# Position attention in a two-layer kernel: softmax in two halves of rows, value products one unit behind score products, later residual sums, pairwise sums in the last turn

## What is computed

```python
qkv = jnp.einsum('sbh,oh->sbo', ln1, qkv_weight)        # 16 query heads, 4 key/value heads, 16 wide
scores = jnp.einsum('bgqsd,bgtd->bgqst', qb, kb) * scale
scores = jnp.where(causal, scores, jnp.finfo(scores.dtype).min)
attn = jax.nn.softmax(scores, axis=-1)
ao = jnp.einsum('bgqst,bgtd->bgqsd', attn, vb)          # s, t in 0..7, t <= s
proj = jnp.einsum('sbh,oh->sbo', ao, proj_weight)
h1 = hidden_states + proj
ln2 = _layer_norm(h1, ln2_weight, ln2_bias)
logits = x @ router_weight
```

## Time and profile before

| | us |
|---|---|
| median of 3 executions | 1807.87 |
| lowest and highest | 1803.91, 1808.4 |
| the profiled execution, its own time | 1806.29 |
| its span in the trace | 1804.5 |
| granted TensorE clock, mean | 0.967 of full speed |
| busy: PE, DVE, ACT, POOL | 92%, 55%, 36%, 28% |

### The profile page before, as it was taken

One profiled execution on the slowest core, in us unless ns is written; L12 is line 12 of the kernel. 1 busy time (PEld: TensorE's weight loads), 2 busy tenths in 40 slices (PEclk: granted clock), 3 DMA queues, 4 the chain that ended last, 5 costly groups with the idle time before them and its releaser, 6 DMA issues. The chain is left out here.

```text
span 1804.5 us, 32036 instructions
## 1 busy us (share of the span) xinstructions
PE 1662.5 (92%) x10572; PEld 1279.3 (71%) x10572; DVE 996.0 (55%) x2525; ACT 643.2 (36%) x1913; POOL 504.8 (28%) x655
## 2 busy tenths in 40 slices
PE   8999899999999978669779999997999997999998
PEld 6777677777778745568768888886666665656555
DVE  6545457787777876895532222215888885322221
ACT  3333255454555465345531111112444443111110
POOL 3222210000000067775153333315455541100000
PEclk9999899999999999889789999999999999999999
DMA  7776500000000000000413233323111100000000
GB/s 192 133 150 114 97 13 13 13 13 13 12 12 1 1 16 1 18 24 28 151 47 100 94 117 94 95 58 100 31 29 30 32 27 1 12 12 12 23 12 24
DMA packets 92268, 88.52 MB, mean 49 GB/s; under 512 B 11456, under 2 KB 82048, under 8 KB 91776
## 3 DMA queue, kind: packets, MB, share of 16 engines
q1 hardware_dynamic: 73392, 56.63, 13.1%
q0 software_dynamic: 6912, 18.88, 3.8%
q10 hardware_dynamic: 11856, 11.66, 1.9%
HBM read 46.64 MB, written 23.20 MB: 39 GB/s over the span
## 5 line engine op out<-in xcount | busy, mean ns | idle before, releaser
L845 ACT ACTIVATE probs<-psS,nm 128x256 f32<-128x256 f32 x256 | 119.1, 470 | 182.5 <-DVE nm L878 182.5
L1764 DVE COPY YE<-e_psY 128x512 f32<-128x512 f32 x40 | 27.7, 692 | 227.7 <-PE e_psY L1712 227.7
L1702 PE MATMUL e_psH<-e_XT,w 128*128 128x256 f32 x640 | 144.8, 379 | 0.0
L1712 PE MATMUL e_psY<-w,e_HT 128*128 128x256 f32 x640 | 144.5, 379 | 0.0
L876 DVE TENSOR_REDUCE mx<-psS 128x2 f32<-128x512 f32 x128 | 87.9, 686 | 84.0 <-PE psS L766 81.7
L1712 PEld LDWEIGHTS e_psY<-w,e_HT 128*128 128x128 f32 x640 | 121.6, 190 | 16.5
L766 PE MATMUL psS<-Rec,QT 128*128 128x256 f32 (+1 forms) x512 | 132.3, 381 | 0.9 <-ACT QT L833 0.9
L1740 ACT ACTIVATE e_HT<-e_psH 128x512 f32<-128x512 f32 x80 | 47.7, 597 | 235.9 <-PE e_psH L1702 235.9
L1702 PEld LDWEIGHTS e_psH<-e_XT,w 128*128 128x128 f32 x640 | 118.6, 190 | 14.5
L1670 POOL DMA_INDIRECT XE<-token_rows,held x80 | 76.0, 950 | 184.6 <-PE e_psX L1689 167.1
L1023 POOL TENSOR_TENSOR prodS<-QKV 128x256 f32<-128x256 f32 x112 | 84.8, 792 | 140.0 <-ACT QKV L1191 113.7
(11 more groups left out here) (285 smaller groups left out, 3559.4 us busy)
## 6 DMA issues: line engine op xcount, KB each, us to landing
KD<-KV SPq DMA_DIRECT2D x256, 66.0 KB, 2.5
expert_out<-YE ACTq DMA_DIRECT2D x40, 256.0 KB, 2.1
w<-in_w SPq DMA_DIRECT2D x16, 512.0 KB, 5.0
X<-in_x SPq DMA_DIRECT2D x8, 512.0 KB, 6.5
x_turned<-XT SPq DMA_DIRECT2D x32, 128.0 KB, 2.3
XS<-x_turned SPq DMA_DIRECT2D x8, 512.0 KB, 4.0
token_rows<-o_XN SPq DMA_DIRECT2D x32, 128.0 KB, 1.7
out_x<-X SPq DMA_DIRECT2D x8, 512.0 KB, 2.9
```

The lines of the kernel that those rows point to most:

```text
L845: nc.scalar.activation(probs[:, b.q % 4, hg, :], psS[b.q % 2][:, hg, :], ACT.Exp, bias=nm[:, b.q % 2, hg:hg + 1], scale=scale, accum_out=s ...
L1702: mm = pe.matmul(psH[c % 2][half][:, m, :], w1[:, s, kc, f:f + P], XT[:, c % 2, kc, :], start=(m == 0 and kc == 0), stop=(m == 1 and kc == ...
L1712: mm = pe.matmul(psY[c % 2][:, j, :], HT[:, c % 2, m, j * P:(j + 1) * P], w2[:, s, m, :], start=(j == 0 and m == 0), stop=(j == 1 and m == ...
```

## The change

It makes five edits, all within `position_attention`.
1. The softmax is done by part. `maxima(i, part)` and `probabilities(j, part)` replace the joint code. Part 0 (rows 0 to 3) of the *entering* tile has its maxima and subtraction at n = 3 of its own turn, its exponential on ACT at s = 3 (in turn 0 at micro step 13), and its probabilities at n = 7. Part 1 keeps its place: maxima after the loop, exponential at s = 6, probabilities at n = 0 of the next turn. The reciprocal becomes two, of 64 elements each.
2. POOL's value unit n stands one unit behind the scores (n = m - 1), and waits for the probabilities of its own part alone.
3. The residual sums of rows 4 and 5 go from the end of the leaving turn to n = 0 of the next one, behind the probabilities.
4. In the last leaving turn (tile 3), `folded` on DVE adds the second half of a value unit to the first, in place, and PE sums only the half that is left: 16 products in place of 28 for rows 0 to 6.
5. The chain's counts (`ENTER`, `LEAVE`, `LAST`) follow.

```diff
@@ -984,7 +984,7 @@
...
-        hs_made = k.sem(ctx, "a_hs_made")
+        hs_made, v_folded = k.sem(ctx, "a_hs_made"), k.sem(ctx, "a_v_folded")
@@ -1050,7 +1050,7 @@
-                for m in range(NU + 3):
+                for m in range(NU + 1):
...
                         ins.then_inc(s_made, 1)
-                    n = m - 3
+                    n = m - 1
                     if leaving and n >= 0:
                         s, t0, t1 = value_units[n]
-                        if n == 0:
-                            pool.wait_ge(p_ready, i * 2)
+                        pool.wait_ge(p_ready, (i - 1) * 2 + (1 if s < S // 2 else 2))
                         pool.wait_ge(v_used, i * NU - NU + n + 1)
@@ -1111,10 +1110,15 @@
                     pe.wait_ge(own_made if own else v_made, j * len(us) + n + 1)
                     src = ownV[:, n, :, :] if own else prodV[:, (j * NU + n) % 3, :, :]
-                    for t in range(t0, t1):
+                    w = t1 - t0
+                    if j == TS - 1 and not own:
+                        pe.wait_ge(v_folded, n + 1)
+                        w = (w + 1) // 2
+                    for t in range(w):
                         for c in range(KC):
-                            mm = pe.matmul(psA[s % 2][:, c, :], src[:, t - t0, c * P:(c + 1) * P], k.ident[:, :],
-                                           start=(t == 0 and c == 0), stop=(t == s and c == KC - 1), skip_group_check=True)
+                            mm = pe.matmul(psA[s % 2][:, c, :], src[:, t, c * P:(c + 1) * P], k.ident[:, :],
+                                           start=(t0 + t == 0 and c == 0), stop=(t1 == s + 1 and t == w - 1 and c == KC - 1),
+                                           skip_group_check=True)
                     mm.then_inc(own_used if own else v_used, 1)
@@ -1190,6 +1194,12 @@
+            def exponential(i, part):
+                s0, s1, t1 = parts[part]
+                act.wait_ge(sub_ready, i * 2 + part + 1)
+                x = PRs[:, i % 2, s0:s1, 0:t1, :].rearrange("p s t h -> p s (t h)")
+                nc.scalar.activation(x, x, ACT.Exp, scale=0.25).then_inc(exp_ready, 1)
@@ -1213,7 +1223,11 @@
+                    if entering and i and s == 3:
+                        exponential(i, 0)
                     for m in micro_steps(i, s):
+                        if i == 0 and m == 13:
+                            exponential(i, 0)
...
                     if entering and s == S - 2:
-                        for part, (s0, s1, t1) in enumerate(parts):
-                            act.wait_ge(sub_ready, i * 2 + part + 1)
-                            x = PRs[:, i % 2, s0:s1, 0:t1, :].rearrange("p s t h -> p s (t h)")
-                            nc.scalar.activation(x, x, ACT.Exp, scale=0.25).then_inc(exp_ready, 1)
+                        exponential(i, 1)
@@ -1284,18 +1295,39 @@
-            def probabilities(j, ch):
+            def folded(j, n):
+
+                s, t0, t1 = value_units[n]
+                w, kept = t1 - t0, (t1 - t0 + 1) // 2
+                x = prodV[:, (j * NU + n) % 3, :, :]
+                dve.wait_ge(v_made, j * NU + n + 1)
+                if w == 1:
+                    dve.sem_inc(v_folded, 1)
+                else:
+                    nc.vector.tensor_tensor(x[:, 0:w - kept, :], x[:, 0:w - kept, :], x[:, kept:w, :],
+                                            ALU.add).then_inc(v_folded, 1)
+
+            def probabilities(j, part, ch):
                 PR = PRs[:, j % 2, :, :, :]
-                for part in range(2):
-                    dve.wait_ge(exp_ready, j * 2 + part + 1)
-                    n = ch.mark(nc.vector.tensor_reduce(each(part)[0], by_t(PR, part), AX.X, ALU.add))
-                ch.after(n)
-                ch.step(nc.vector.reciprocal(mx[:, :, :], mx[:, :, :]))
-                for part in range(2):
-                    row, shape = each(part)
-                    nc.vector.tensor_tensor(by_t(PR, part), by_t(PR, part), bc(row.unsqueeze(3), shape),
-                                            ALU.mult).then_inc(p_ready, 1)
-                dve.wait_ge(p_ready, j * 2 + 2)
+                row, shape = each(part)
+                dve.wait_ge(exp_ready, j * 2 + part + 1)
+                ch.step(nc.vector.tensor_reduce(row, by_t(PR, part), AX.X, ALU.add))
+                ch.step(nc.vector.reciprocal(row, row))
+                nc.vector.tensor_tensor(by_t(PR, part), by_t(PR, part), bc(row.unsqueeze(3), shape),
+                                        ALU.mult).then_inc(p_ready, 1)
+                dve.wait_ge(p_ready, j * 2 + part + 1)
+
+            def maxima(i, part, ch):
+                PR = PRs[:, i % 2, :, :, :]
+                row, shape = each(part)
+                dve.wait_ge(s_summed, i * NU + (4 if part == 0 else NU) + 3)
+                ch.step(nc.vector.tensor_reduce(row, by_t(sc, part), AX.X, ALU.max))
+                if i >= 2:
+                    dve.wait_ge(v_made, (i - 1) * NU)
+                    dve.wait_ge(own_made, (i - 1) * NO)
+                nc.vector.tensor_tensor(by_t(PR, part), by_t(sc, part), bc(row.unsqueeze(3), shape),
+                                        ALU.subtract).then_inc(sub_ready, 1)
+                dve.wait_ge(sub_ready, i * 2 + part + 1)
@@ -1327,7 +1359,7 @@
-            ENTER, LEAVE, LAST = S + NO + 2, S - 2 + 3, 2 + 6 + 1
+            ENTER, LEAVE, LAST = S + NO + 2 + 2, S - 4 + 2, 4 + 6 + 1
@@ -1348,35 +1380,29 @@
                     if leaving and n == 0:
-                        probabilities(i - 1, ch)
+                        probabilities(i - 1, 1, ch)
+                    if last and n == 0:
+                        for s in (S - 4, S - 3):
+                            add(i - 2, s, ch)
...
                     if last and n == 2:
                         statistics(i - 2, ch)
+                    if entering and n == 3:
+                        maxima(i, 0, ch)
+                    if entering and n == 7:
+                        probabilities(i, 0, ch)
                     if leaving and n in own_value_at:
                         own_value(i - 1, own_value_at[n])
                     if last and not leaving and n >= 2:
                         chosen(n - 2)
+                    if leaving and not entering:
+                        folded(i - 1, n)
                     if leaving and n in add_at:
                         add(i - 1, add_at[n], ch)
                 if entering:
-                    dve.wait_ge(s_summed, i * NU + NU + 3)
...
-                    dve.wait_ge(sub_ready, i * 2 + 2)
-                if leaving:
-                    add(i - 1, 4, ch)
-                    add(i - 1, 5, ch)
+                    maxima(i, 1, ch)
                 assert ch.n == ENTER * entering + LEAVE * leaving + LAST * last, ch.n
```

More of the change, by code:

```diff
@@ L1363, in turn @@
                 if entering:
-                    dve.wait_ge(s_summed, i * NU + NU + 3)
-                    for part in range(2):
-                        m = ch.mark(nc.vector.tensor_reduce(each(part)[0], by_t(sc, part), AX.X, ALU.max))
-                    ch.after(m)
-                    PR = PRs[:, i % 2, :, :, :]
-                    if i >= 2:
-                        dve.wait_ge(v_made, (i - 1) * NU)
-                        dve.wait_ge(own_made, (i - 1) * NO)
-                    for part in range(2):
-                        row, shape = each(part)
-                        nc.vector.tensor_tensor(by_t(PR, part), by_t(sc, part), bc(row.unsqueeze(3), shape),
-                                                ALU.subtract).then_inc(sub_ready, 1)
-                    dve.wait_ge(sub_ready, i * 2 + 2)
-                if leaving:
-                    add(i - 1, 4, ch)
-                    add(i - 1, 5, ch)
+                    maxima(i, 1, ch)
                 assert ch.n == ENTER * entering + LEAVE * leaving + LAST * last, ch.n
```

## The result

The changed kernel takes 1794.99 us (median of 6 runs, 1794.66 to 1798.61), the kernel before 1806.61 us (6 runs, 1802.67 to 1808.4). The ratio is 0.9945, 95% interval [0.9935, 0.9955]: **faster by 0.55%**. By that ratio the gain is 9.9 us (8.1 to 11.7), by the medians 11.6 us. The forecast of 1793.9 lies 1.1 us from the median. The profiled execution took 1796.49 us, span 1794.7, mean granted clock 0.968. Against the profiled execution before (1806.3) that is 9.8 us, where the sum said 14.

What follows compares the result with a forecast made beforehand. DVE, fed by POOL, was taken to bound turns 2 and 3, PE turn 4. Gains 3.9 + 5.4 + 3.0 + 3.2 = 15.5, less 1.5, gave 14 us: 1806.3 to 1792.3, plus 1.6 for the median, 1793.9; range 1786 to 1806.

Steps and rivals of the forecast that it cites:

- B: From turn 2's last DVE statistics row to turn 3's own value products: 9.2 us gained less 3.8 charged, 5.4 us.
- A: Up to DVE's last statistics row of turn 2: 3.9 us gained, 3.5 at turn 1's end and 0.4 in turn 0.
- D: Turn 4 behind its statistics mark: PE sums 12 products fewer, 5.8 us, of which 3.2 us were taken as gain.
- C: From turn 3's own value products to turn 4's last DVE statistics row: 7.3 us gained less 4.3 charged, 3.0 us.
- a product of 512 elements, 1.0: DVE's product in part 1's probabilities at the start of turn 2, priced at 1.0 us like a large subtraction.
- the +0.4 for turn 0: Part 0's maxima and subtraction leave turn 0's end: between 1.2 us gained and 0.8 lost, taken as +0.4.
- rival 1: POOL's unbroken runs lock DVE out of softmax operations in turns 1 to 3 and folds, 7.2 us each; chance 0.2.
- The own value products now meet POOL as well: DVE's own value products slow down beside a working POOL: 4 x 0.49 us, written as 1.8 and charged in full.
- 7.2 us of standing in the subtractions and the 2 us for row 3: DVE's waits in turn 2's subtractions and before row 3's residual sum, claimed gone between the marks of turns 2 and 3.
- Rival 3: Folding in turn 4 pays nothing since PE waits for folds: D is 0, 1797 us; chance 0.1.
- I take 1.5 for waits of DVE on POOL: Deduction of 1.5 us from the summed gain of 15.5 for DVE's waits on POOL that the rows can't show.
- Rival 2: DVE then waits for POOL or PE: turns 2 and 3 fall to 46 us only, 1799 us; chance 0.2.

Runs made afterwards that it cites:

- run 11: Changed kernel with one POOL pause in turn 2, behind unit 1's score products, some 3 us before the product by probabilities: 1793.21 us, ratio 0.9926.
- run 12: Changed kernel with one POOL pause in turn 2, ahead of its first score unit, some 5 us before the product by probabilities: 1793.31 us, ratio 0.9925.
- run 4: Changed kernel with value units put back to three units behind the scores, all else kept: 1799.82 us, ratio 0.9967.
- run 5: Kernel before with only the residual sums of rows 4 and 5 moved behind the next turn's probabilities: 1804.42 us, ratio 0.9994.
- run 7: Kernel before with only the folding of value units in the last leaving turn: 1802.46 us, ratio 0.998.
- run 6: Changed kernel with the residual sums of rows 4 and 5 back at the end of their own turn: 1795.93 us, ratio 0.9942.
- run 3: Changed kernel without folding, so PE sums all 28 value products in the last turn: 1797.42 us, ratio 0.9958.
- run 8: Changed kernel with POOL waiting for its own score products before each value unit, in every turn: 1794.34 us, ratio 0.9924.
- run 10: Kernel of run 9 with the residual sums of rows 4 and 5 back at the end of their own turn: 1795.79 us, ratio 0.9946.
- run 9: Changed kernel with POOL waiting for its own score products before each value unit, in turn 2 alone: 1792.13 us, ratio 0.9925.
- run 2: Changed kernel with POOL waiting in turn 2, before score unit 3, until part 1's probabilities are made: 1792.06 us, ratio 0.9929.

## Why the prediction was right, and where it was not

The total was right, and partly by luck. Of its four terms B came near the mark, A and D were too high, and C was too low.

**A failed, at the step "a product of 512 elements, 1.0".** It cost 5.88 us, 4.9 more than priced, and 3.9 - 4.9 = -1.0 is near the -1.4 measured. The rest is the +0.4 for turn 0, which was not seen: row 7's sums of turn 1 start 92.9 us behind the stage's start, before 92.6. All else before that step stands: the sum began at 724.46 against 724.3. With the stall gone (runs 11 and 12) A is +2.1 and +1.2 us. Then 1.8 and 2.7 us are missing up to 3.9. Of them 1.9 us are the statistics chain, which the sum had carried over unchanged: from its first row to the mark it took 2.8 us before, and takes 4.7 us in both runs. The prediction knew the 7 us lock-out and named it rival 1, with a list of places: part 0's subtraction and product, part 1's subtraction, and the folds. It came at none of them (longest 1.54 us), and once at a place that is not on the list, the product of part 1 at the start of turn 2. The rival's price of 7.2 us was 4.9, since the row ended with POOL's stop. Its opposing argument, that POOL may run only three score units ahead, agrees with a stall that ends, but did not exclude it. The prediction also took POOL's run at 765 to begin at 761.1. The trace of before has no gap in it from 745.52 on, so the length of POOL's run alone could not have told where DVE will stand.

**B, 5.4 against 4.7, by two errors that offset.** "The own value products now meet POOL as well" was charged with 4 x 0.49, which the prediction writes as 1.8 (it is 1.96), and was mostly not paid: behind turn 2's mark 4 of them take 1.84 us where it was 1.42. That is 1.4 us better. Statistics rows of 0.17 us that meet POOL at 0.5 to 0.75 us were in no term: from the chain's first row to the mark 2.8 us before, 4.7 after, 1.9 us worse. 5.4 + 1.4 - 1.9 = 4.9. The main step, "7.2 us of standing in the subtractions and the 2 us for row 3" gone, holds: the subtraction of part 1 takes 1.54 us, and no row waits for PE in that stretch. The reason given in passing, "the POOL row of 13 value products becomes 7", isn't what does it: run 4 has the 13 products in one go and no stall there. Edits 3 and 4 alone (runs 5 and 7) leave rows of 8.79 and 8.80 us in place; run 4, without edit 2, and run 6, without edit 3, don't have them. What these two share for turns 2 and 3 is edit 1 (edit 4 is at work in turn 4 only). It puts the product of part 0 some 4 us ahead of the subtraction. Edit 1 alone was not run.

**C, 3.0 against 4.8** (3.6 in the second profile). The same 1.8 us for own values was charged again, and again not paid: at turn 3's mark 4 of them take 1.43 us, 0.36 each, as before. 4.8 would have been the sum. Its other terms hold: waits for PE fell from 6.1 to 1.9 us (5.6 were counted as gone), the wait on ACT's square root rose from 2.5 to 3.1 (0.5 charged), the exponential cost 0.8 (0.6 charged). Run 4, where C is lost, says that the lag of one unit carries it.

**D, 3.2 against 1.2** (1.8 in the second profile). "nearer to the PE figure since POOL may be three units ahead when the mark falls" was the wrong side to lean to. POOL's chain from the mark to its last product took 17.5 us (16.8 before and in run 3, without folds), and folds hold it: 0.72 us a product where 0.58 was read. Row 7's sums came 9.3 us earlier than before, not the 15 that the prediction gave as its sign. Run 3 and run 7 give 1.2 and 1.7 us by the marks; by the medians run 3 gives 1.9 and by the ratio run 7 gives 3.6, with an interval of 1.8 to 5.4 that holds the 3.2 too. The PE work saved, 5.8 us, was work that stood beside POOL's. Rival 3, a gain of zero, is excluded by run 7's interval.

**"I take 1.5 for waits of DVE on POOL"**: they did not come in turns 2 and 3. DVE waited for POOL at the end of turn 1 (4.2 us for score unit 0) and in turn 4's folds (2.4 us in all). The 1.5 stood in for part of the stall without naming it, and 9.3 against 14 is what was left.

**Why the total came out right all the same.** Against the profiled executions the sum was 4.2 us too good: 1792.3 where 1796.49 was measured. The forecast then added 1.6 us, since in the kernel before the median lay above the profiled execution; in the changed kernel the median lies 1.5 us below it. Those two make up 3.1 of the 4.2 us, and 1.1 us is left. Neither has to do with the mechanism: this is luck, and by the ratio, whose 9.9 us are near the 9.8 of the profiles, the gain was some 4 us under the 14 forecast.

**Rival 2's price** does not follow from the marks. A period of 46 us would be 2.2 us less than B's 48.2, but 2.5 us more than the 43.5 that C already had, so no gain of 3.5. The periods came out at 43.6 and 38.8 us.

**Rule and row.** The rule in the Trainium skill, page "SBUF — State Buffer", section "Who interferes with whom", is that the shared port is held for the whole instruction and the other engine blocks until then. Rows between 1.08 and 1.61 us for the product in runs 6 and 8 to 12 agree with it, as do the statistics rows of 0.5 to 0.75 us against 0.17: one instruction of POOL's is waited for. The 5.88 us row doesn't: eight of POOL's instructions ran to their end in it. The same product, against the same instructions in the same order, did either, as run 12 shows. The prediction costed by the rule where the trace had already shown the exception once.

**Edit 3** was worth nothing alone (run 5), nothing on top of the rest while the stall stood (run 6 against the changed kernel, by the ratios), and some 2.6 us, by the estimate above, once it was gone (run 10 against run 9).

## What to carry to other kernels

Where two engines that keep each other out of SBUF both have work in reach, removing a wait on one joins the other's runs: before taking out a wait, look at what it breaks up. Ahead of each two-input operation read two things: how long the other engine has run without a gap, and how long ago this engine last got in with such an operation. Every stand of 3 us or more here had over 7 us of the one and over 8 us of the other, but not every such meeting led to a stand. An operation that takes 5 times its own length is a place to try a pause of 0.2 us on the other engine. One pause 3 to 5 us ahead was enough here.

## What was new about the hardware

DVE's two-input product of 128x512 (about 1.0 us alone) took, at the start of turn 2, by how long POOL had run without a gap when it was issued:

| POOL unbroken for | product | product's end behind POOL's stop |
|---|---|---|
| 0.2 to 1.4 us (runs 8, 9, 6, 10) | 1.27, 1.28, 1.61, 1.61 us | POOL works on |
| 3.1 us (run 11) | 1.08 us | POOL works on |
| 5.1 us (run 12) | 1.09 us | POOL works on |
| 7.1 us (after) | 5.88 us | 0.87 us |
| 7.1 us (run 4) | 3.03 us | 0.89 us |
| 7.1 us (run 2) | 1.43 us | 0.90 us |

The three last ended at a constant distance from the stop, whatever made POOL stop, and the 5.88 repeated as 5.88 and 5.90 us in the changed kernel's rerun and in run 3. In all of these DVE's last two-input operation lay 8 us or more back. So at this place, between 5.1 and 7.1 us of unbroken work, something changes from "one instruction is waited for" to "DVE waits until POOL stops". Time is one reading; the number of POOL's finished instructions in the run (7 in run 12, 10 or 11 in the others) is as good, and neither was told from the other. In turn 2 of the kernel before, DVE's last own product ended 8 us ahead of the subtractions, and they stood until POOL's stop at 772.8. In run 2's statistics chain, rows get in within 0.76 us though POOL had not paused for 9 us and more; DVE's own score products lie 4 us ahead of them. At the end of turn 2 of the changed kernel the product of part 1 takes 1.04 us, 18.7 us into POOL's run and 2.4 us behind DVE's subtraction. That such a meeting restarts the count, as a pause does, is argued from these rows and was not tried.

And some rows do not fit. In turn 3 of the kernel before, the subtractions (3.33 us) met a POOL without a gap for 19.8 us and came 8.1 us behind the last meeting, as in turn 2; yet they ended at 816.95 while POOL ran on to 817.9. In run 7 they stood at the same place, after the same number of POOL's products, for no more than one instruction each (2.12 us for both), where in turn 2 of the same run they took 8.80. So the long run and the long absence make a stand possible and do not decide it, and being kept out doesn't always last until POOL stops. What decides stays open.

Turn 1's granted clock (674 to 728) was 0.95 in some kernels and 0.91 in others (runs 2, 4, 5, 10), and where it was lower the rows of its end came about 2 us later, in run 2 without an edit that touches them. What sets it stays open; marks of turn 2 compare to 1 to 2 us only.
